# An LSTM over 1024 positions: the input projection made piece by piece inside the loop

## What is computed

```python
scale = 1.0 / np.sqrt(256)
ys = y * scale                                   # y = cond, [2, 256]
d = rsqrt(einsum('bi,io->bo', ys * ys, weight * weight) + EPS)
x = x + einsum('bsi,io->bso', x * ys[:, None, :], weight) * d[:, None, :]   # x: [2, 1024, 256]
xW = einsum('ntd,dk->tnk', x, Wx) + b            # Wx: [256, 1024]
def step(carry, xw_t):                           # 1024 steps, batch 2
    prev_h, prev_c = carry                       # h0 = cond, c0 = 0
    a = xw_t + prev_h @ Wh                       # Wh: [256, 1024]
    i, f, o, g = sigmoid(a_i), sigmoid(a_f), sigmoid(a_o), tanh(a_g)
    next_c = f * prev_c + i * g
    next_h = o * tanh(next_c)
x = x + hs
```

## Time and profile before

| | us |
|---|---|
| median of 3 runs | 2076.16 |
| lowest, highest | 2069.64, 2078.4 |
| the profiled execution's own time | 2075.25 |
| its span, first to last instruction | 2073.5 |

### The profile page before, as it was taken

How to read it: one execution, slowest core, us unless ns; L and a number is a source line. 1 busy time by engine, 2 the same in 40 slices (tenths; PEclk the granted TensorE clock), 3 DMA queues, 4 the chain that set the end, 5 groups by cost and what they waited for, 6 DMA issues and landing times.

```text
span 2073.5 us, 140158 instructions
## 1 busy us (share of the span) xinstructions
PE 1876.1 (90%) x57580; PEld 1735.6 (84%) x57580; DVE 1269.7 (61%) x8384; ACT 689.4 (33%) x4125; POOL 498.7 (24%) x1291
## 2 busy tenths in 40 slices
PE   9999999999999999999999999999999999999997
PEld 5588888888888888888888888888888888888887
DVE  3366666666666666666666666666666666666665
ACT  2233333333333333333333333333333333333333
POOL 1122222222222222222222222222222222222221
PEclk9855555555555555555555555555555555555555
DMA  2000000000000000000000000000000000000000
GB/s 86 2 1 1 1 1 1 1 1 1 1 1 1 1 1 1 1 1 1 1 1 1 1 1 1 1 1 1 1 1 1 1 1 1 1 1 1 1 1 1
DMA packets 20368, 6.67 MB, mean 3 GB/s; under 512 B 17532, under 2 KB 19848, under 8 KB 20360
## 3 DMA queue, kind: packets, MB, share of 16 engines
q1 hardware_dynamic: 20088, 6.30, 1.2%
q10 hardware_dynamic: 272, 0.26, 0.0%
HBM read 4.46 MB, written 2.10 MB: 3 GB/s over the span
## 4 chain that ended last, share of the span: by engine, by line
PE 75%; DVE 10%; ACT 9%; issue 5%; DMA 0%; SPq 0%; POOLq 0%; POOL 0%; DVEq 0%
PE psum L295 75%; DVE psum L586 10%; ACT scan_in L663 9%; PE psum L318 0%; DMA small_rows<-in_L_cond_b_dram 0%; ACT xw L642 0%; DVE w L468 0%; SPq L185 0%; POOLq L56 0%; PE psum L300 0%; POOL y_cols L246 0%; DVE y_rows L600 0%; DVE y_rows L605 0%; DVE h_parts L589 0%; DVE ys L464 0%
## 5 line engine op out<-in xcount | busy, mean ns | idle before, releaser
L295 PE MATMUL psum<-h_parts,wh_p 128*128 128x2 f16 (+1 forms) x45056 | 1370.4, 166 | 0.0
L295 PEld LDWEIGHTS psum<-h_parts,wh_p 128*128 128x128 f16 x45056 | 1286.5, 104 | 16.2
L295 PE MATMUL psum<-ring,ident_b 128*128 128x4 bf16 (+2 forms) x12288 | 491.2, 168 | 186.2 <-DVE psum L586 184.7
L295 PEld LDWEIGHTS psum<-ring,ident_b 128*128 128x128 bf16 x12288 | 407.4, 105 | 271.0 <-DVE psum L586 268.6
L660 ACT ACTIVATE sig_f<-psum 128x4 f32<-128x4 f32 x1024 | 178.3, 174 | 1127.1 <-DVE psum L577 1127.1
L577 DVE TENSOR_REDUCE psum<-psum 128x4 f32<-128x8 f32 x1024 | 178.9, 175 | 389.2 <-PE psum L295 389.2
L234 POOL CAST ring<-xw 128x64 bf16 (+1 forms) x256 | 120.7, 471 | 1148.5 <-POOLq L272 1124.0
L589 DVE SCALAR_TENSOR_TENSOR h_parts<-scan_h 128x4 f16<-128x4 f32 x1024 | 175.9, 172 | 247.7 <-ACT scan_h L667 247.7
L665 ACT ACTIVATE scan_h<-psum 128x4 f32<-128x4 f32 x1024 | 180.2, 176 | 142.2
L592 DVE TENSOR_TENSOR_SCAN h_parts<-scan_h,h_parts 128x12 f16<-128x12 f32 x1024 | 188.0, 184 | 35.1
L579 DVE TENSOR_REDUCE psum<-psum 128x4 f32<-128x8 f32 x1024 | 179.1, 175 | 39.7
(11 more groups left out here) (74 smaller groups left out, 155.9 us busy)
## 6 DMA issues: line engine op xcount, KB each, us to landing
out_dram<-y_rows SPq DMA_DIRECT2D x512, 4.0 KB
x_rows<-in_x_dram SPq DMA_DIRECT2D x4, 512.0 KB, 6.9
wh_sb<-in_L_cond_Wh_dram SPq DMA_DIRECT2D x1, 1024.0 KB, 10.2
wx_sb<-in_L_cond_Wx_dram SPq DMA_DIRECT2D x1, 1024.0 KB, 11.9
w_sb<-in_L_cond_weight_dram ACTq DMA_DIRECT2D x1, 256.0 KB, 2.8
small_rows<-in_cond_dram SPq DMA_DIRECT2D x1, 2.0 KB
small_rows<-in_L_cond_b_dram SPq DMA_DIRECT2D x1, 4.0 KB
```

The source lines that it names most:

```text
L295: return nc.tensor.matmul(out_, lhs, rhs, start=first, stop=last, skip_group_check=True)
```

## The change

The projection before the loop makes only the first 17 of 128 pieces (a piece is one chunk of 128 outputs, one batch row and 128 positions; 16 pieces cover 128 positions). Each of the other pieces is made in the loop, one a turn, 17 turns ahead of the first that could need it, as twelve bf16/fp16 matmuls of 128 columns: Wx in two parts and x in three, for both halves of the contraction, added up in PSUM bank 6. Two of them stand in each of the steps 3 to 8 of a turn, one after f's input matmuls and one after o's. f's input matmuls now wait for sigmoid f of the step before (f_act) and not for the scan. SP copies the piece's operands, from SBUF to SBUF, to fixed places (stage) when the last matmul of the piece before is done. ScalarE reads the finished piece after the eighth step's tanh, adds the bias and writes it to xw. GpSimd splits x into three parts, eight positions a turn, 34 turns ahead, behind the first half's save, and its turn begins with a wait for the piece read a turn before. Before the loop there is new work: the largest value of Wx and its scales on VectorE, Wx's copies on ScalarE and its second part on GpSimd, and the first 144 positions of x past the first 128 split on VectorE; the first layer of the second half of x comes after the 17 pieces. The ScalarE read of pieces before the loop is gone, and VectorE reads all 17. The core of the diff:

```diff
+FIRST_PIECE = 2
+LEAD = 17
+AHEAD = 2 * LEAD
...
-        xw = sb("xw", [P, M, B, T])
+        xw = sb("xw", [P, NI, P])
+        wx_s = sb("wx_s", [P, K, G * D])
+        wx_p = sb("wx_p", [P, 2, K, G * D], F16)
+        x_p = sb("x_p", [P, 3, K, B, T], BF16)
+        wx_piece = sb("wx_piece", [P, 2, K, P], F16)
+        x_piece = sb("x_piece", [P, 3, K, P], BF16)
+        x_rest = sb("x_rest", [P, K, B, AHEAD * UNROLL - P])
...
-        groups += [(("scales",), "dve"), (("h0wh",), "dve")]
-        groups += [(("xw", b, m, n), "act" if m % 2 else "dve") for n in range(NB) for b in range(B) for m in range(M)]
...
-            with sp.Fori(0, NI) as i:
+
+            def stage(turn):
+
+                if isinstance(turn, int):
+                    item = (turn + LEAD) % NI
+                    weights, rows = ((item // B) % M) * P, (item % B) * T + (item // ITEMS) * P
+                else:
+                    item = sp.snap((turn + LEAD) % NI)
+                    weights = sp.snap(((item // B) % M) * P)
+                    rows = sp.snap((item % B) * T + (item // ITEMS) * P)
+                sp.dma_start(wx_piece[:, :, :, :].rearrange("p w k n -> p (w k) n"),
+                             wx_p[:, :, :, bass.ds(weights, P)].rearrange("p w k n -> p (w k) n")).then_inc(x_staged, 16)
+                sp.dma_start(x_piece[:, :, :, :].rearrange("p q k n -> p (q k) n"),
+                             x_p[:, :, :, :, :].rearrange("p q k b t -> p (q k) (b t)")[:, :, bass.ds(rows, P)]).then_inc(x_staged, 16)
+
+            def store(turn):
+
+                for q in range(stores):
+                    sp.dma_start(out_t[q, :, bass.ds(turn * (UNROLL * K), UNROLL * K), :],
+                                 y_rows[q * QUAD:(q + 1) * QUAD, :]).then_inc(s_out, 16)
+
+            sp.wait_ge(s_wx_hi, 1)
+            sp.wait_ge(s_wx_lo, 1)
+            sp.wait_ge(x_split, 1)
+            stage(0)
+            with sp.Fori(0, NI - 1) as i:
+                sp.wait_ge(x_split, i + 2)
+                sp.sem_inc(store_seen, 1)
+                sp.wait_ge(x_mm, i + 1)
+                sp.sem_inc(store_seen, 1)
+                stage(i + 1)
                 sp.wait_ge(y_turned, i + 2)
                 sp.sem_inc(store_seen, 1)
-                for q in range(stores):
-                    sp.dma_start(out_t[q, :, bass.ds(i * (UNROLL * K), UNROLL * K), :],
-                                 y_rows[q * QUAD:(q + 1) * QUAD, :]).then_inc(s_out, 16)
+                store(i)
+            sp.wait_ge(y_turned, NI + 1)
+            store(NI - 1)
...
+            pool.wait_ge(s_wx_hi, 1)
+            pool.wait_ge(s_wxs, 1)
+            nc.gpsimd.tensor_tensor(wx_p[:, 1, :, :], wx_s[:, :, :], wx_p[:, 0, :, :], ALU.subtract).then_inc(s_wx_lo, 1)
...
             with pool.Fori(0, NI - 1) as i:
                 t = i * UNROLL
+                t_x = pool.snap(((i + AHEAD) % NI) * UNROLL)
+                now = xt[:, :, :, bass.ds(t_x, UNROLL)].rearrange("p k b t -> p (k b) t")
+                part = [x_p[:, q, :, :, bass.ds(t_x, UNROLL)].rearrange("p k b t -> p (k b) t") for q in range(3)]
+                pool.wait_ge(x_read, i + 1)
+                pool.sem_inc(pool_seen, 1)
                 for half in range(2):
+                    done = t + (half + 1) * HALF
+                    src = xw_source(half, i + 1)
                     pool.wait_ge(ring_used, 1)
                     pool.sem_inc(ring_used, -1)
-                    split(half, t + UNROLL + half * HALF)
-                    pool.wait_ge(h_all, t + (half + 1) * HALF)
-                    pool.sem_inc(pool_seen, 1)
+                    split_high(half, src)
+                    split_rest(half, src)
+                    split_middle(half)
+                    split_low(half)
+                    after_step(done)
                     if half == 0:
                         pool.wait_ge(y_turned, i + 1)
                         pool.sem_inc(pool_seen, 1)
                     save(half, t + half * HALF)
+                    if half == 0:
+                        nc.gpsimd.tensor_copy(part[0], now).then_inc(s_pool, 1)
+                        settle()
+                        nc.gpsimd.tensor_tensor(res, now, part[0], ALU.subtract).then_inc(s_pool, 1)
+                        settle()
+                        nc.gpsimd.tensor_copy(part[1], res).then_inc(s_pool, 1)
+                        settle()
+                        nc.gpsimd.tensor_tensor(part[2], res, part[1], ALU.subtract).then_inc(x_split, 1)
...
+            for v in range(LEAD):
+                block, m, b = v // ITEMS, (v // B) % M, v % B
+                bank = start_group(("xw", v))
+                for k in range(K):
+                    last = mm(bank[:, 0:P], wx_sb[:, k, m * P:(m + 1) * P], xt[:, k, b, block * P:(block + 1) * P], k == 0, k == K - 1)
+                last.then_inc(s_filled, 1)
+            for n in range(1, NB):
+                project_x(n, range(B))
...
+                terms = [(k, w_part, x_part) for k in range(K) for w_part in range(2) for x_part in range(3)]
+
+                def project(n):
+
+                    k, w_part, x_part = terms[n]
+                    return mm(banks[X_BANK][:, 0:P], wx_piece[:, w_part, k, :], x_piece[:, x_part, k, :], n == 0, n == len(terms) - 1)
+
+                done = 0
                 for u in range(UNROLL):
                     if u % HALF == 0:
                         pe.wait_ge(ring_full, 2 * i + u // HALF + 1)
+                    if u == FIRST_PIECE:
+                        pe.wait_ge(x_staged, 32 * i + 32)
+                        pe.wait_ge(x_read, i + 1)
+                    pe.wait_ge(f_act, t + u + 1)
+                    input_apart(GATE_F, u, 0, K)
+                    if u >= FIRST_PIECE:
+                        project(done)
+                        done += 1
                     pe.wait_ge(c_done, t + u + 1)
-                    input_apart(GATE_F, u, 0, K)
                     input_apart(GATE_G, u, 0, K)
                     input_together(GATE_I, I_BANK, u, 0, K)
                     pe.wait_ge(o_act, t + u + 1)
@@ -435,6 +541,11 @@
                     last = input_together(GATE_O, O_REST, u, 1, K)
                     if u % HALF == HALF - 1:
                         last.then_inc(ring_used, 1)
+                    if u >= FIRST_PIECE:
+                        last = project(done)
+                        done += 1
+                        if done == len(terms):
+                            last.then_inc(x_mm, 1)
                     pe.wait_ge(h_hi, t + u + 1)
                     products(GATE_I, I_BANK, 0, 0, K)
...
+            dve.wait_ge(s_wx, 16)
+            dve.wait_ge(s_wx2, 1)
+            nc.vector.tensor_reduce(wmax[:, 1:2], wx_sb[:, :, :], AX.XY, ALU.max, apply_absolute_value=True).then_inc(s_wmax, 1)
...
+            soon = slice(P, AHEAD * UNROLL)
+            link(nc.vector.tensor_copy(x_p[:, 0, :, :, soon], xt[:, :, :, soon]))
+            link(nc.vector.tensor_tensor(x_rest[:, :, :, :], xt[:, :, :, soon], x_p[:, 0, :, :, soon], ALU.subtract))
+            link(nc.vector.tensor_copy(x_p[:, 1, :, :, soon], x_rest[:, :, :, :]))
+            nc.vector.tensor_tensor(x_p[:, 2, :, :, soon], x_rest[:, :, :, :], x_p[:, 1, :, :, soon], ALU.subtract).then_inc(x_split, 1)
...
+            def read_xw(v):
+
+                bank = group(("xw", v))
+                m = (v // B) % M
+                nc.vector.tensor_scalar(xw[:, v, :], bank[:, 0:P], scales[:, 0:1], bias_s[:, m:m + 1], ALU.mult, ALU.add).then_inc(s_dve, 1)
+
+            for v in range(LEAD):
+                read_xw(v)
+            dve.wait_ge(*read_out(order[("xw", ITEMS - 1)]))
+            nc.vector.scalar_tensor_tensor(out=xw[:, 0:ITEMS, 0], in0=h0wh[:, :, :].rearrange("p m b -> p (m b)"), scalar=scales[:, 0:1],
+                                           in1=xw[:, 0:ITEMS, 0], op0=ALU.mult, op1=ALU.add).then_inc(s_start, 1)
+            for n in range(1, NB):
+                add_projection(n, range(B))
...
+            nc.scalar.activation(wx_p[:, 0, :, :], wx_sb[:, :, :], ACT.Copy, scale=scales[:, 2:3]).then_inc(s_wx_hi, 1)
+            nc.scalar.activation(wx_s[:, :, :], wx_sb[:, :, :], ACT.Copy, scale=scales[:, 2:3]).then_inc(s_wxs, 1)
+            load_tables()
...
+                    if u == UNROLL - 1:
+
+                        act.wait_ge(x_mm, i + 1)
+                        act.sem_inc(act_seen, 1)
+                        nc.scalar.activation(xw[:, bass.ds(item, 1), :].rearrange("p n t -> p (n t)"), banks[X_BANK][:, 0:P], ACT.Identity,
+                                             bias=bias_s[:, bass.ds(chunk, 1)], scale=x_unit[:, :]).then_inc(x_read, 1)
```

More of the change, by code:

```diff
@@ L157, in cond_resid_lstm @@
             groups += per_bank("xt", n)
-        groups += per_bank("x1", 0) + [(("wmax",), "dve")]
+        groups += per_bank("x1", 0) + [(("wmax",), "dve"), (("h0wh",), "dve"), (("scales",), "dve")]
+        groups += [(("xw", v), "dve") for v in range(LEAD)]
```

(48 more changed lines are left out.)

110 lines of the change are left out of this document (63 added, 47 removed).

## The result

| | before | after |
|---|---|---|
| median, us (4 runs each) | 2076.39 | 2039.72 |
| lowest, highest | 2069.64, 2078.4 | 2038.61, 2040.31 |
| profiled execution, its span | 2075.25, 2073.5 | 2039.63, 2037.8 |

The ratio is 0.983, with a 95% interval of 0.981 to 0.985: faster by 1.7%. The forecast was 2033, the range 2015 to 2085.

What follows compares the result with a forecast made beforehand. The prediction took tanh and h_hi, not the input matmuls, as the path from scan to products in steps of 1.93 us. Sum: 2073.5 - 46 + 4 + 1.75 = 2033 us, range 2015 to 2085.

Steps and rivals of the forecast that it cites:

- part 1: Projection before the loop: 17 pieces instead of 32 groups move the first load from 88.6 to 42.3, gaining 46 us.
- part 2: Twelve wide matmuls a turn in the loop: hidden in two idle stretches of TensorE's step, cost 0.
- part 3: SP's staging copies inside SBUF: landed at 4.6 us, 0.9 us early for the third step, so nothing lost.
- part 4: ScalarE's read of a finished piece after the eighth step's tanh: 0.03 us a turn, 4 us in all.
- part 5: GpSimd's added work in a turn: 7 of 15.4 us busy, halves made early, nothing waits, cost 0.
- the bound from fp32: Wide matmul in the second idle stretch at fp32's 0.22 us: 0.10 late, six times a turn, 79 us in all.
- Rival C: Second wide matmul of a step does not fit: 0.03 us six times a turn, 23 us, 2056; chance 0.07.
- Rival A: Staged operands land late, 4.3 us after issue: third step waits 0.65 us each turn, 83 us, total 2116; chance 0.15.
- rival B: ScalarE's turn end decides: 0.25 us a turn, 28 us more than in the sum, 2061; chance 0.10.
- Rival D: Wide matmuls bring TensorE's clock back to 2.4 GHz in the loop: 56 us less, 1977; chance 0.05.

Runs made afterwards that it cites:

- the third copy: Changed kernel with a third staged copy a turn, the weights' piece again to an unread place, TensorE waiting for all three: 2085.62 us, ratio 1.006.
- With three increments: Changed kernel with three empty semaphore increments before each of GpSimd's two splits a turn: 2025.62 us, ratio to the kernel before 0.977.
- before, 3 increments: Kernel before with three empty semaphore increments ahead of each of GpSimd's splits, nothing else of the change: 2112.04 us, ratio 1.020.
- changed, 6 increments: Changed kernel with six empty semaphore increments ahead of each of GpSimd's splits: 2062.13 us, ratio to the kernel before 0.996.

## Why the prediction was right, point by point

| term, us | predicted | measured |
|---|---|---|
| part 1, first load of the loop | -46 | -45.1 |
| part 2, wide matmuls | 0 | 0 |
| part 3, staging | 0 | 0 |
| part 4, ScalarE's turn end | +4 | 0 |
| part 5, GpSimd | 0 | +13.7, and +1.5 in the eighth step |
| level of the undisturbed steps | 0 | -5 |
| behind the loop | 0 | -0.7 |

The time was in the range and the main gain right. Two terms were wrong, part 4 and part 5; that the sum is only 7 us off is in part luck, as 15 us unforeseen stand against the 4 of part 4 that never came and the 5 of the level.

**Part 1** holds step by step. VectorE's 17 reads took 6.31 us (6.3 predicted), TensorE's second first-layer block ended at 33.88 + 7.03 = 40.9 (40.3), GpSimd's first half was split by 39.50 + 0.50 = 40.0 (40.8). TensorE, not GpSimd, was last, as said. The first load is 1.2 later than 42.3: 0.6 of it is there at the block's end. From the end of the memset that releases the loop (42.54 + 0.07) to the load it is 0.9 us; in the kernel before it was 0.5. By the code, counters that TensorE used to bring up to date ahead of that wait now stand behind it, and in the trace these three increments run from 42.8 to 43.1. No run without them was made. The first scan of the versions with the same prologue lies between 44.6 and 46.8, so 1 us here is no more than what executions differ by.

**Part 2** holds in its times. A step with wide matmuls, changed kernel, loads and matmuls:

```profile
505.73 0.34 PEld L386 LDWEIGHTS psum<-ring,ident_b 128*128 128x128 bf16 x10 [0.18 <-DVE psum L709]
...
506.02 0.27 PE L386 MATMUL psum<-x_piece,wx_piece 128*128 128x128 bf16 x1
...
506.14 1.25 PEld L386 LDWEIGHTS psum<-h_parts,wh_p 128*128 128x128 f16 x44
```

From the first of the ten inputs the wide one starts at 0.29 and the products at 0.41, as worked out. So the wide one takes the engine for at most 0.12 us, and the bound from fp32 (0.22) does not apply. Its record is 268 ns against 166 for the narrow ones, 0.10 us for 126 more columns, which fits the assumed column a cycle at 1.2 GHz; but ends of matmuls are modelled, so the starts are the better witness. The Trainium skill, "TensorE: Matmul & The Clock Gate", section "Back-to-back issue gap", gives N / 1.2 ns, 107 ns here; the trace's 0.12 or less agrees. Rival C (2056) is false by the run without these matmuls. By the estimate it was close: 0.29 + 0.107 leaves some 0.01 us.

**Part 3** came to the right cost by wrong steps, and with luck. The landing was right (2.7 against 2.6), the issue was not: SP's four stores end at 508.20, in the eighth step, and not "2 us ahead of the next staging". The last wide matmul starts at 507.95 and ends by its record at 508.21; SP's branch, waits and address work begin only behind the stores, and x's copy goes out at 510.19, 2.5 into the eighth step and not 2.0. The room is 0.12 us to the f inputs and 0.33 to a loss, not 0.9. Rival A begins at a landing 0.33 later than the measured one, not 1.0 later as my figures had it. The landing of 4.3 us that it supposed did not come true, but its chance of 0.15 was worked out against a margin three times too wide. The Trainium skill, "DMA: Bandwidth & Descriptors", section "Why small descriptors are slow (HBM only)", exempts copies inside SBUF from the penalty that "Specifications" of the same page gives for transfers under 512 B. The 2.7 us for 192 KB in runs of 256 B fit the exemption; no run here has a copy of the same size in longer runs, so that it holds is not shown.

**Part 4**: the read's size was off, and its cost too. ScalarE at the end of turn 40:

```profile
680.48 0.18 ACT L789 ACTIVATE scan_h<-psum 128x4 f32<-128x4 f32 x1
680.96 0.46 ACT L794 ACTIVATE xw<-psum,bias_s,x_unit 128x128 f32 x1 [0.30 <-issue]
681.76 0.17 ACT L782 ACTIVATE sig_f<-psum 128x4 f32<-128x4 f32 x1 [0.35 <-DVE psum L700]
```

The read takes 0.46, not 0.32, but it starts 0.48 after the tanh and not at 0.60, and the sigmoid of f comes 1.28 after the tanh, against 1.27; it was waiting for VectorE, for 0.35. The wait for the last wide matmul, from which the 0.60 came, is long over by then: in the turn of part 3 this matmul starts at 507.95 and the tanh of the eighth step at 509.56. Ahead of the read stands only work of ScalarE's own queue, and the branch and the counters fit in too. The 4 us are not there, and rival B (2061) is false.

**Part 5** is the term that failed. "Nothing waits: 0" was argued from GpSimd's own time and from how early its halves are needed. Both are true. What I left out is that the split's operations moved by 0.18 us against VectorE's ring, and that GpSimd and VectorE get in each other's way without any semaphore between them. The subtract's 0.28 us lead could be read in the trace of before, and the added address work in the diff. The Trainium skill states the rule, on the page "SBUF — State Buffer", section "Who interferes with whom": a VectorE instruction with two inputs from SBUF contends with a GpSimd one that reads SBUF, and whichever starts first has the shared pair of ports. The runs agree on who is held; that it is a port they can't show. By rows of before alone, a scan held for at most the subtract's 0.35 us, once or twice a turn, would have been a rival at 2033 + 45 to 2033 + 90.

The 0.012 of the eighth step goes with a meeting of the same kind. There a cast of GpSimd, which has one input, starts 0.07 to 0.08 ahead of the scan that makes the low part of h:

```profile
680.82 0.48 POOL L297 CAST ring<-rest 128x64 bf16<-128x64 f32 x1 [0.17 <-POOLq L279]
680.89 0.19 DVE L715 TENSOR_TENSOR_SCAN h_parts<-scan_h,h_parts 128x12 f16<-128x12 f32 x1
```

I took the mean of this scan in the eighth step for each trace. It is 0.194 in the changed kernel, 0.193 with the third copy and 0.191 without wide matmuls, and the eighth step is 0.012, 0.010 and 0.009 too long. With three increments, which move the cast, it is 0.183 and the excess 0.002.

**Rival D** (1977) is false: clock 0.50 in the window above. The sum with the measured terms and without part 5 would have been 2073.5 - 45.1 - 0.7 + 1.75, some 2029, less up to 5 for the level: 2024 to 2029. The version with three increments, which has the whole change and not the collision, measured 2025.62.

## What to carry to other kernels

When an edit moves GpSimd's work by a tenth of a microsecond, list what VectorE is doing at that moment, and the other way round; "it has plenty of time" covers waits on semaphores and nothing else. In a profile the sign of it is an instruction whose minimum and median are as ever and whose maximum isn't (191/192/312), at one place of the turn. And before an idle stretch elsewhere in a queue is counted as spare, follow that queue through the whole turn: what was taken for 0.9 us was 0.12.

## What the runs showed of the hardware

The hold-up has a fixed shape. In the steps shown of four runs a VectorE instruction with two SBUF inputs began 0.04 to 0.10 us after GpSimd's 64-column subtract, and taking its undisturbed length (0.19 scan, 0.17 high part) off its end, it was let go at nearly the same time after the subtract's start:

| run | instruction begins after the subtract | its length | let go after the subtract's start |
|---|---|---|---|
| before, 3 increments | 0.04 | 0.35 | 0.20 |
| changed, 6 increments | 0.06 | 0.32 (high part) | 0.21 |
| changed, no wide matmuls | 0.09 | 0.29 | 0.19 |
| changed | 0.10 | 0.30 | 0.21 |
| before | 0.28 | 0.19 | not held |
| changed, 3 increments | -0.14 | 0.19 | not held |

The subtract's own record is 0.34 to 0.35 in all of them. Over all meetings of these four runs and of the one with the third copy, some 870, the median of the last column is 0.20 in each run. So the subtract holds the other for about 0.2 us from its start and not for all of its record. The Trainium skill, page "SBUF — State Buffer", section "Who interferes with whom", has "for the whole instruction"; GpSimd's spans in a profile are rough, though, and that its real work ends there fits as well.

It takes no second input on GpSimd's side. A cast that had run for 0.29 us when the scan began had no effect on it, in the changed kernel with six increments. But one that has only just begun holds an instruction with two SBUF inputs as well, for a shorter time: the low part above is let go about 0.09 after the cast's start. In the version with three increments VectorE's product for hring starts 0.04 to 0.09 behind the cast in the fourth and the eighth step, takes 0.20 instead of 0.15 and is let go at 0.11 to 0.13:

```profile
675.92 0.47 POOL L297 CAST ring<-rest 128x64 bf16<-128x64 f32 x1 [0.17 <-POOLq L279]
...
675.98 0.20 DVE L721 TENSOR_TENSOR hring<-scan_h 128x4 f32<-128x4 f32 x1
```

Nothing on the critical path waits for this product, so it costs no time there.

The other surprise is small: an empty increment of a semaphore on GpSimd takes 0.08 us (three of them moved the cast from 0.76 to 0.52 ahead of the scan, and in the kernel before from 0.94 to 0.70), which makes them a fine adjustment for such a collision.
